# A graph network's last layer carried out within the second step's program, shared by four engines

## What is computed

```python
h = relu(layernorm(x))
S = adj + I;  Rf = S / rowsum;  Rb = S / colsum
Xf = Xb = Xa = h;  Z = 0
for s in range(2):                       # step one, step two
    A  = nucleus(Xa @ W1 @ W2 @ (Xa @ W3).T, 0.9)   # softmax over the largest logits
    Xf, Xb, Xa = Rf @ Xf, Rb @ Xb, A @ Xa
    Z += Xf @ U1[s] + Xb @ U2[s] + Xa @ U3[s]
x1 = x + layernorm(h + Z) * gamma + beta
h2 = relu(layernorm(x1))
out = x1 + sum_heads softmax(q k.T/8 + 0.01 I - 1e16 (1 - max(adj, I))) @ (h2 @ Wv) @ Wo
```

## Time and profile before

| | us |
|---|---|
| time, median of 3 runs (lowest, highest) | 2463.35 (2461.59, 2464.17) |
| time of the profiled execution | 2464.38 |
| its span, first to last instruction | 2462.6 |
| PE busy | 2189.1 (89%) |
| DVE busy | 2061.0 (84%) |
| ACT busy | 1947.4 (79%) |
| POOL busy | 714.1 (29%) |
| mean granted TensorE clock, share of full | 0.938 |

### The profile page before, as it was taken

One profiled execution on the slowest core, in us unless ns is written; L12 is line 12 of the kernel. 1 busy time (PEld: TensorE's weight loads), 2 busy tenths in 40 slices (PEclk: granted clock), 3 DMA queues, 4 the chain that ended last, 5 costly groups with the idle time before them and its releaser, 6 DMA issues. The chain is left out here.

```text
span 2462.6 us, 26021 instructions
## 1 busy us (share of the span) xinstructions
PE 2189.1 (89%) x8302; PEld 1438.0 (58%) x8302; DVE 2061.0 (84%) x3884; ACT 1947.4 (79%) x2813; POOL 714.1 (29%) x921
## 2 busy tenths in 40 slices
PE   7599999999999996999499999999999999999846
PEld 4377777677777775444255555555555556555535
DVE  5699999999999995444699999999999999999743
ACT  5899999999999992233889989898998989989423
POOL 2133344333344330000033332333423333233200
PEclk9699999999999998999799999999999999999868
DMA  5334455434444432321012122212212122121141
GB/s 174 91 90 108 111 120 120 101 100 107 114 120 119 95 76 74 81 64 54 28 36 51 49 42 61 41 49 51 53 49 41 49 53 51 49 43 47 27 133 56
DMA packets 77981, 183.19 MB, mean 74 GB/s; under 512 B 11665, under 2 KB 57872, under 8 KB 77840
## 3 DMA queue, kind: packets, MB, share of 16 engines
q1 hardware_dynamic: 56800, 125.48, 16.0%
q0 software_dynamic: 18720, 54.53, 13.1%
q10 hardware_dynamic: 2320, 1.48, 0.2%
HBM read 154.19 MB, written 27.28 MB: 74 GB/s over the span
## 5 line engine op out<-in xcount | busy, mean ns | idle before, releaser
L1440 DVE SCALAR_TENSOR_TENSOR s_junk<-s_logits,s_small,s_expd 128x3327 uint8<-128x3327 f32 x208 | 766.4, 3685 | 5.5
L947 PE MATMUL bank<-h_aug,s_attT 128*128 128x256 f32 x2704 | 635.6, 384 | 1.2 <-ACT s_attT L1178 1.2
L923 PE MATMUL bank<-both,s_adj 128*128 128x512 f32 x1352 | 609.9, 596 | 28.8 <-ACT s_sides_out L1199 28.7
L947 PEld LDWEIGHTS bank<-h_aug,s_attT 128*128 128x128 f32 x2704 | 513.2, 193 | 115.0 <-issue 47.6
L923 PEld LDWEIGHTS bank<-both,s_adj 128*128 128x128 f32 x1352 | 251.5, 190 | 305.1 <-issue 260.6
L923 PE MATMUL bank<-h_aug,s_adj 128*128 128x257 f32 x1352 | 353.5, 413 | 27.7 <-ACT s_spread_out L1185 27.7
L923 PEld LDWEIGHTS bank<-h_aug,s_adj 128*128 128x128 f32 x1352 | 270.3, 206 | 116.9 <-ACT s_spread_out L1185 46.1
L1115 ACT ACTIVATE s_junk<-s_expd,s_small 128x3327 int8<-128x3327 f32 x104 | 319.8, 3075 | 2.8 <-POOL s_small L1285 1.7
L1109 ACT ACTIVATE s_junk<-s_expd,s_small 128x3327 int8<-128x3327 f32 x104 | 319.2, 3069 | 1.8
L911 PE MATMUL bank<-KTr,QT 64*128 64x512 f32 (+1 forms) x728 | 234.8, 629 | 60.5 <-DVE s_logits L1374 47.9
L1178 ACT ACTIVATE s_attT<-bank 128x512 f32<-128x512 f32 (+1 forms) x364 | 192.0, 563 | 106.0 <-PE bank L937 91.2
(11 more groups left out here) (219 smaller groups left out, 2668.7 us busy)
## 6 DMA issues: line engine op xcount, KB each, us to landing
s_adj<-adj_turned SPq DMA_DIRECT2D x104, 832.0 KB, 5.3
s_adj_total<-adj_turned POOLq DMA_DIRECT2D x52, 832.0 KB, 7.4
z<-s_sides_out POOLq DMA_DIRECT2D x52, 128.0 KB, 3.2
spread<-s_spread_out SPq DMA_DIRECT2D x26, 128.5 KB, 2.9
m_spread_in<-spread SPq DMA_DIRECT2D x26, 128.5 KB, 2.2
attended<-s_att_out SPq DMA_DIRECT2D x26, 128.0 KB, 5.4
m_att_in<-attended SPq DMA_DIRECT2D x26, 128.0 KB, 2.2
z<-m_z_out SPq DMA_DIRECT2D x26, 128.0 KB, 1.7
```

The lines of the kernel that those rows point to most:

```text
L923: done = pe.matmul(SX[:, 0:width], half(t, h)[:, bass.ts(jj, P)], rows_of(j), start=(j == 0), stop=(j == T - 1))
L947: last = pe.matmul(AB[:, 0:D], attT[i % 4][:, b, :], h_aug[:, g + b, 0:D], start=(g + b == 0), stop=(g + b == T - 1))
L1440: chain.did(dve.scalar_tensor_tensor(junk[:, 0:N], logits[t % 3][:, 0:N], col(t, "cand"), expd[t % NE][:, 0:N], ALU.is_gt, ALU.mult, accum ...
```

## The change

The second layer's short path leaves `second_layer` and goes into step two's own block, so that there is no barrier, no clearing and no reload between them. `second_layer` now holds the general path alone: SP waits there for the last stores, each engine loads the flag and jumps over it.

- **Where it lives.** z, x, the turned rows and the outputs take buffers that step two no longer needs: the exponentials of tile T-2, the keys (`KTr`), the queries (`QT`, for the statistics) and the adjacency products' operand `both` (from its last use on).
- **Loads.** SP loads z and x by groups within step two: groups 0 and 1 once tile T-2 is kept, groups 2 to 5 once PE has used the last adjacency half, group 6 once the last tile's attention is added to `z`.
- **Weights.** `Wvo` is made at the start of step one: ACT issues the two loads, PE multiplies after the first tile's `spread`, ACT copies.
- **The join.** It was two passes of DVE per tile. Now ACT scales and shifts z (`scale_own`), POOL multiplies by gamma and adds x (`weight_own`, two instructions per group).
- **The output.** The product with the identity is gone from PE and the copy from ACT; DVE adds `x1` while it reads PSUM (`add_own`).
- **The last tile of both steps.** DVE makes the lifted copy itself (`lift_last`), into the buffer of tile T-3, at the same time as ACT counts ties; `keep_last` writes the kept weights in two parts, 1536 and 1792 columns, and PE may start on the first three groups after part one (`LAST_PART = 3`).
- **Order.** The statistics of z and the own scaling run three groups ahead of the rest.

Cut to its core and moved 12 columns to the left (`turn_last`, `store_last`, `lift_last`, `find_flag` and `scale_of` do as told above or as their like before):

```diff
...
-def choose(eng, general, identity):
-    eng.wait_ge(sem["flag_ready"], 1)
+def choose(eng, general):
     taken = eng.value_load(flag_int[0:1, 0:1], min_val=0, max_val=2)
     with eng.If(taken > 0):
         general()
-    with eng.Else():
-        identity()
...
+    for i in range(2):
+        sp.wait_ge(out_stored[i], s.stores_of(i))
+    choose(sp, general)
 @block.gpsimd
...
                 act.wait_ge(sem["g_oT"], n + 1)
                 act.activation(oT[:, :], banks[5][0:KD, 0:P], ACT.Copy).then_inc(sem["g_oT_stored"], 1)
-    def identity():
-        act.wait_ge(sem["wvo_done"], 1)
-        act.activation(wvo[:, :, :], banks[6][:, :].rearrange("q (k d) -> q k d", k=KT), ACT.Copy
-                       ).then_inc(sem["wvo_stored"], 1)
...
                 store_attended(t - 1)
+        if not first_step:
+            sp.wait_ge(sem["logits_done"], T * NC)
+            sp.dma_start(gamma_b, gamma.partition_broadcast(P)).then_inc(sem["gamma_loaded"], 16)
+            for g, (t, w) in enumerate(s.GROUPS):
+                if g == 0:
+                    sp.wait_ge(sem["kept_ready"], T - 1)
+                if g == 2:
+                    sp.wait_ge(sem["adj1_used"], T)
+                for i in range(2):
+                    sp.wait_ge(sem[f"att_added{i}"], 16 * ((t + w + 1 - i) // 2))
+                sp.dma_start(z_rows(g), z_d[t:t + w, :, :].rearrange("t p d -> p t d")
+                             ).then_inc(sem[f"z_loaded{g}"], 16)
+                sp.dma_start(x_rows(g), xb_d[t:t + w, :, :].rearrange("t p d -> p t d")
+                             ).then_inc(sem[f"x_loaded{g}"], 16)
+            for g, (t, w) in enumerate(s.GROUPS):
+                sp.wait_ge(sem["out_ready"], 2 * g + (w + 1) // 2)
+                whole_tiles = min(w, N // P - t)
+                sp.dma_start(out[t * P:(t + whole_tiles) * P, :].rearrange("(t p) d -> p t d", p=P),
+                             out_rows(g)[:, 0:whole_tiles, :]).then_inc(out_stored[g % 2], 16)
+            rest = T - 1 - s.GROUPS[-1][0]
+            sp.dma_start(out[(T - 1) * P:N, :], out_rows(NG - 1)[0:N - (T - 1) * P, rest, :]
+                         ).then_inc(out_stored[(NG - 1) % 2], 16)
         if first_step:
             store_attended(T - 1)
...
                 pe.wait_ge(sem["kept_ready"], t + 1)
+            if t == T - 1 and n == LAST_PART:
+                pe.wait_ge(sem["kept_ready"], T + 1)
             if i >= NTB:
...
+        def last_weights():
+            pe.wait_ge(sem["w_loaded"], 32)
+            for k in range(KT):
+                for i in range(HC):
+                    last = pe.matmul(banks[7][:, bass.ts(k, D)], wvT[:, i, bass.ts(k, P)], wo[:, i, :],
+                                     start=(i == 0), stop=(i == HC - 1))
+            last.then_inc(sem["wvo_done"], 1)
+        def turn_last(g):
+            t, w = s.GROUPS[g]
+            pe.wait_ge(sem["h_ready"], g + 1)
+            if g >= 2:
...
+        def multiply_last(g):
+            t, w = s.GROUPS[g]
+            pe.wait_ge(sem["hT_stored"], g + 1)
+            for half in range((w + 1) // 2):
+                q = 2 * g + half
+                if q == 0:
+                    pe.wait_ge(sem["spread_read"], T)
+                if q == 3:
+                    pe.wait_ge(sem["att_read"], T)
+                if q >= 4:
+                    pe.wait_ge(sem["out_ready"], q - 3)
...
+                    for k in range(KT):
+                        done = pe.matmul(OUTS[q % 4][:, bass.ts(i % 2, D)], hT_of(g)[:, k, bass.ts(i, P)],
+                                         wvo[:, k, :], start=(k == 0), stop=(k == KT - 1))
+                done.then_inc(sem["out_done"], 1)
...
             if t == 0:
                 for n in range(NG):
                     spread(0, n)
+                if first_step:
+                    last_weights()
                 make_logits(1, range(NC))
...
+        if not first_step:
+            pe.wait_ge(sem["found_ready"], 1)
+            pe.matmul(banks[2][0:1, 0:2], ones_col[:, :], found[:, :], start=True, stop=True
+                      ).then_inc(sem["found_summed"], 1)
+            for g in range(NG):
+                turn_last(g)
+                if g > 0:
+                    multiply_last(g - 1)
+            multiply_last(NG - 1)
     @block.scalar
...
+        def store_weights():
+            act.wait_ge(sem["wvo_done"], 1)
+            act.activation(wvo[:, :, :], banks[7][:, :].rearrange("q (k d) -> q k d", k=KT), ACT.Copy
+                           ).then_inc(sem["wvo_stored"], 1)
+            act.wait_ge(sem["wvo_stored"], 1)
...
+        def scale_own(g):
+            t, w = s.GROUPS[g]
+            act.wait_ge(sem["own_norm_ready"], g + 1)
+            for i in range(w):
+                last = act.activation(z_rows(g)[:, i, :], z_rows(g)[:, i, :], ACT.Identity,
+                                      bias=shift[0][:, t + i:t + i + 1], scale=rstd[0][:, t + i:t + i + 1])
+            last.then_inc(sem["own_scaled"], 1)
...
+        if first_step:
+            act.dma_start(wvT[:, :, :], WvT.rearrange("(c p) d -> p c d", p=P)).then_inc(sem["w_loaded"], 16)
+            act.dma_start(wo[:, :, :], Wo.rearrange("h k d -> (h k) d").rearrange("(c p) d -> p c d", p=P)
+                          ).then_inc(sem["w_loaded"], 16)
         act.wait_ge(sem["constants_set"], 5)
         store_logits(0, range(copied))
...
             if first_step:
+                if t == 0:
+                    store_weights()
                 if following:
                     store_logits(t + 1, (0, 1))
                 if previous:
                     count_ties(t - 1)
                 if following:
                     store_logits(t + 1, range(2, copied))
-                if previous:
+                if previous and present:
                     lift(t - 1)
                 if following:
...
                 if previous:
                     read_attended(t - 1)
             else:
-                if previous:
+                if previous and present:
                     read_sides(t - 1)
                     count_ties(t - 1)
                     lift(t - 1)
+                if not present:
+                    count_ties(T - 1)
+                    read_sides(T - 1)
+                    find_root(0, 0, "own_var_ready", "own_root_ready")
                 if following:
                     store_logits(t + 1, range(NC))
                 if t > 1:
@@ -1263,10 +1307,27 @@
                     guess(t + 1)
                     probe(t + 1, 0, lambda: turned(3), lambda: turned(4))
                     probe(t + 1, 1, lambda: turned(5, 6), nothing)
+                elif present:
+                    turned(3, 4, 5, 6)
                 else:
-                    turned(3, 4, 5, 6)
-                if not present:
+                    scale_own(0)
+                    turned(3)
+                    find_root(0, 1, "own_var_ready", "own_root_ready")
+                    scale_own(1)
+                    turned(4, 5, 6)
+                    find_root(0, 2, "own_var_ready", "own_root_ready")
+                    scale_own(2)
                     scale_attended(T - 1)
+                    for g in range(NG):
+                        if g + 3 < NG:
+                            find_root(0, g + 3, "own_var_ready", "own_root_ready")
+                        find_root(1, g, "var_ready", "root_ready")
+                        if g + 3 < NG:
+                            scale_own(g + 3)
+                        if g > 0:
+                            store_last(g - 1)
+                        rectify(g)
+                    store_last(NG - 1)
     @block.gpsimd
...
                 add_columns(t)
+        def weight_own(g):
+            w = s.GROUPS[g][1]
+            pool.wait_ge(sem["own_scaled"], g + 1)
+            if g == 0:
+                pool.wait_ge(sem["gamma_loaded"], 16)
+            pool.tensor_tensor(z_rows(g), z_rows(g), gamma_b.unsqueeze(1).to_broadcast([P, w, D]), ALU.mult
+                               ).then_inc(sem["own_weighted"], 1)
+            pool.wait_ge(sem["own_weighted"], g + 1)
+            pool.wait_ge(sem[f"x_loaded{g}"], 16)
+            pool.tensor_tensor(x_rows(g), x_rows(g), z_rows(g), ALU.add).then_inc(sem["x1_ready"], 1)
         if not first_step:
+            for g in range(3):
+                weight_own(g)
             add_attended(T - 1)
-            for i in range(2):
-                pool.wait_ge(sem[f"att_added{i}"], 16 * (T // 2))
+            for g in range(3, NG):
+                weight_own(g)
     @block.vector
...
                                      ALU.mult, accum_out=col(t, "n_gt")).then_inc(sem["larger_summed"], 1)
+        def lift_last():
+            dve.wait_ge(sem["turned"], (T - 2) * NG)
...
+            chain.wait()
+            chain.did(dve.reciprocal(col(t, "inv"), col(t, "total")))
+            chain.did(dve.tensor_scalar(col(t, "sharetau"), col(t, "count"), col(t, "invties"), col(t, "tau"),
```

(43 more changed lines are left out.)

264 lines of the change are left out of this document (133 added, 131 removed).

## The result

The changed kernel takes **2402.2 us** (median of 4 runs, 2400.98 to 2406.72) against 2462.47 us of the kernel before (4 runs beside it): ratio 0.9759, 95% interval 0.9742 to 0.9776, so 60.3 us less. The forecast was 2411 us in a range of 2400 to 2428. The profiled execution took 2400.98 us, span 2399.2.

The account below looks back on a forecast made before the run. Latency was taken to bound the last layer, no engine being full, with serial waits at step two's end. Those parts gave -51.3, step one -3.0 and +1.5: -52.8 from 2463.35, given as 2411 us, range 2400 to 2428.

Parts of the forecast that it names:

- a: Step two's end: DVE lifts the last tile (3.68 us) and keeps it in parts; PE starts 3.8 us earlier.
- g: Tail after the last rectify: PE's products, DVE's addition, stores issued by 2403.1, landing 7.0 us later; end at 2411.3.
- h: Step one: PE starts 3.0 us earlier at its last tile; loads and weights at its start cost 1.5 us.
- c: Flag after the last attention: PE's sum, 0.2 us, and five small DVE instructions, 0.8 us; done at 2346.4.
- d: First rectify of the last layer, after measures, root, scale (0.8 us) and own scaling: 2355.3 against 2385.2 before.
- e: Groups 1 to 3 of the last layer: ACT is the serial engine, 6.9 us per group, 19.7 in all.
- f: Groups 4 to 6: a ring through PE, DVE and ACT over two groups, 13.2 us; 18.8 in all.
- Rival 3: DVE waits for POOL's whole product at each scale, 3.5 us more in three turns: 2421 us; chance 0.08.
- rival 1: Shorter pauses keep PE at full clock: last attention saves 2.6 us, groups 4 to 6 save 2; 2403 us; chance 0.15.
- Rival 2: PE at half clock throughout the last layer, 9.0 us a group, 12.4 later: 2423 us; chance 0.12.
- Rival 4: No overlap: loads or the flag hold the last layer until after the last attention; 2448 us; chance 0.03.
- Rival 5: Slower than before: POOL's products far dearer than 2.35 us, the crossing point being 8.2 us each; chance 0.02.

Follow-up runs that it names:

- old_tail: The changed kernel with the end of both steps put back (ACT lifts the last tile after its count, DVE keeps it in one instruction): 2406.94 us.
- split_store: The changed kernel with the last store of 127 rows made as two, of 112 and 15 rows: 2402.4 us.
- weights_twice: The changed kernel with PE's sixteen matmuls for the weights product at the start of step one issued twice: 2405.28 us, one run.
- late_start: The changed kernel with the last layer's loads and first work held until the last attention is added to z, so no overlap: 2423.64 us.
- join_dve: The changed kernel with the join of the own rows given back to DVE, without ACT's scaling and POOL's two products: 2407.2 us.

## Why the prediction was right, and where its steps were off

The span fell by 63.4 us: 56.6 behind the point in step two, 6.8 ahead of it. The forecast had 51.3 (a to g) and 1.5 (h). In local times, the forecast's ends less 2319.37:

| step | forecast | measured |
|---|---|---|
| a. PE starts | 8.4 | 7.7 |
| b. last attention ends | 26.0 | 24.8 |
| c. flag done | 27.0 | 27.4 |
| d. first rectify ends | 35.9 | 35.3 |
| e. fourth rectify ends | 55.6 | 54.8 |
| f. last rectify ends | 74.4 | 69.9 |
| g. last issue ends | 83.7 | 78.4 |
| span ends | 91.9 | 86.6 |

**a** was mis-sized in two parts, and they partly cancelled. The pass took 1.95 us and not the 3.68 that I took from a pass with two inputs. The rule cited from "VectorE: DVE Perf Modes" gave half, and the trace agrees with the rule. That alone would have put PE at 7.1, by my sum. But DVE then waited 1.0 us for `settled`, which I had called not waited for. POOL's first small step was held for 1.83 us beside the pass (0.19 elsewhere); without that POOL would have been ready about 0.55 us earlier (an estimate from its rows: its steps would then have waited for ACT's count), and this is the way from 7.1 to 7.7.

**c** missed the hold: the flag's addition took 1.83 us instead of 0.15. With the 1.2 us gained by the end of b the two nearly come out even. old_tail showed the same from the other side: there PE's sum came 1.1 us later and the hold was 1.2 shorter, and the first rectify stood where it was.

**d** took 1.0 us less than its sum, 0.4 of it since its scales fell beside no product.

**e** is right in its total, 19.5 us against 19.7, but not in its chain, and that is luck. I had made ACT the serial engine, at 6.9 a group. Only the first interval was ACT's, and it took 5.6. The next two, 13.9 together, went through PE's turn at the lower clock (1.97 us) and its product (4.43), DVE's addition and the measures behind it: the ring that I had set for f alone. The hold was in the sum as 0.44 us per scale, a mean of four from the earlier trace rows; in truth it is 0 or up to 2.3 us as a scale falls beside a product or not. Rival 3 had each scale held for a whole product; 3 shifts of 14 were held for 1.2 to 2.2 us, and with a tighter order 8 of 14 for 0.4 to 2.3.

**f** is the step that failed most: 15.1 us measured where 18.8 stood. Its sum of 13.2 has 4.3 us for the product. From the fourth rectify's end to the sixth's the chain was the one that I had set, in 11.8 us: turn 2.0, product 4.1, addition and measure 2.4, root 0.2, copies 1.1, rectify 2.0. PE was no quicker in it than forecast, since the turn at 2367.47 ran at the lower clock. What I had wrong is that the scale (0.8) and the copies (1.2) stood in line, where DVE scales while ACT copies. The last half group took 3.2 us and not 5.6: its rectify waited for PE's turn (1.09) and the copies. The product, addition and measure, which the ring would have put in its way, were done in time, the last addition at 2377.89 and the measure right behind it. Of rival 1, b had 0.5 of its 2.6 us (the rest of b's gain is a's), f at most 0.6 of its 2, the last turn at 1.09 for 1.7. The rest was open to be had: in split_store, where PE stayed at full clock, f took 13.6 us.

**g** took 8.5 us where 9.3 stood. Behind it, last issue to span's end, 8.2 us were forecast and 8.2 measured, and that is luck: SP waited 5.7 us for the store and not 7.0, and what comes after took 2.5 and not 1.2.

**h** had the right size for step one's end in this execution: 26.76 us from the last sum to the copied attention before, 23.86 after, 2.9 against 3.0. Only 2.2 of it is PE's earlier start (9.91 to 7.72), which I had put at 3.0; the rest varies from one execution to the next, 23.5 to 25.0 us over the eleven. Its other term, 1.5 us for the weights at the start, was wrong: nothing of ACT's copy, issues or PE's products shows by more than 0.3 us (weights_twice). The remaining 3.9 of the 6.8 us came in no edit's place: 1.7 us were there by the first probe already, where PE's clock rose earlier in the first block (the first product there took 2.43 us instead of 3.62), 1.6 arose within step one and 0.6 behind it. Eleven executions with this step one have the middle of their arrivals at 2316.1, 3.2 ahead of before's. That is close to h without its 1.5; but before has one trace only, of an execution 1.9 us above its median. So of the 7.5 us between forecast (52.8) and measurement (60.3), 5.3 are the last layer (f 3.7, d 1.0, g 0.8, a 0.7, b 0.5, e 0.2, less 1.6 in c), 1.5 the weights, and 0.7 is less than executions differ.

Rival 2 (half clock throughout) did not come: the later products took 3.62 us, with a granted clock of 0.93 over the last stretch. Rival 4 did not come either; late_start, which takes the overlap away, cost 19 to 21 us, not 37. Rival 5 needed 8.2 us a product; those of four tiles took 2.34 to 2.37. Against the rule on the join, the decision was right and the price wrong: 3 to 5 us, not 19. I had charged 2.9 us to each of 6.5 groups. In join_dve the first three intervals between rectifies grew by 1.6, 0.2 and 0.7 us and the other three by 0.2 together, for behind the third no own rows are left to join, and before it DVE has no additions to make.

## What to carry to other kernels

Where a layer hangs on a ring of engines, look first at the order on each queue: placing each part where its data are ready, with shifts that POOL can't hold, gave 17.9 us more (PE's kept clock included), nearly what the whole overlap (19 us) was worth. When work moves to an empty engine, list which instructions of the others it can hold, and give the small ones on the critical chain a form with one tensor input. And count a gain to the next wait only: most of a quicker store, and all of an earlier flag and of step two's earlier keep, were gone by the waits behind them.

## What the runs showed that was not expected

- A hold ends with the other engine's instruction: DVE instructions of 0.16 us that began beside a POOL product lasted up to 2.3 us, to its end each time; DVE statistics and column shifts beside the same products kept their time, and so did additions with one input from PSUM (0.69 us).
- It works both ways: the 1.95 us pass on DVE made a POOL instruction of 0.19 us last 1.83.
- SP waited 5.7 us for a store of 127 rows of 1 KB; one of 112 rows landed in 1.9.
- Executions with the same instructions up to there reach the last sum of step two up to 6.5 us apart (2312.60 to 2319.10).
